# First layer's attention: normalisation and scaling moved to GpSimd, the roots gathered in two slots

## What is computed

```python
xn = layernorm(x) * gamma
q, k, v = split(xn @ w_q, xn @ w_kv)          # 16 heads of 64
k, v = concat(null_k, k), concat(null_v, v)   # two null keys in front
q = q / max(norm(q), 1e-12) * q_scale
k = k / max(norm(k), 1e-12) * k_scale
sim = 8 * q @ k.T + alibi, causal
out = softmax(sim) @ v                        # per head
return concat_heads(out) @ w_out
```

## Time and profile before

| | us |
|---|---|
| median of 3 runs | 2028.43 |
| lowest and highest | 2022.0, 2038.33 |
| the profiled execution | 2043.86 |
| its span from first to last instruction | 2042.1 |

### The profile page before, as it was taken

One profiled execution on the slowest core, in us unless ns is written; L12 is line 12 of the kernel. 1 busy time (PEld: TensorE's weight loads), 2 busy tenths in 40 slices (PEclk: granted clock), 3 DMA queues, 4 the chain that ended last, 5 costly groups with the idle time before them and its releaser, 6 DMA issues. The chain is left out here.

```text
span 2042.1 us, 35995 instructions
## 1 busy us (share of the span) xinstructions
PE 1633.4 (80%) x13931; PEld 819.6 (40%) x13931; DVE 1223.0 (60%) x2150; ACT 886.8 (43%) x1438; POOL 764.7 (37%) x423
## 2 busy tenths in 40 slices
PE   2468459879889898898989998345998889888887
PEld 2246325435354353544535443224654323333232
DVE  5323357686766757576576661481266877777761
ACT  0112215536456463564635455012322655555566
POOL 1500553564656656465564768260000111400000
PEclk9879759989899998999989999567998977888888
DMA  4113210000000000000000000123320000000000
GB/s 156 52 32 107 48 24 12 7 12 22 7 19 11 18 17 7 24 12 12 17 7 20 12 12 12 65 79 94 93 74 27 13 13 28 9 18 2 2 7 17
DMA packets 57109, 62.00 MB, mean 30 GB/s; under 512 B 12890, under 2 KB 42862, under 8 KB 56046
## 3 DMA queue, kind: packets, MB, share of 16 engines
q1 hardware_dynamic: 52846, 51.32, 8.1%
q0 software_dynamic: 4096, 8.40, 1.6%
HBM read 40.34 MB, written 18.48 MB: 29 GB/s over the span
## 5 line engine op out<-in xcount | busy, mean ns | idle before, releaser
L1582 POOL TENSOR_TENSOR a_prob_sum<-a_prob_sum,a_prob 128x1024 f32<-128x1024 f32 (+2 forms) x224 | 499.9, 2232 | 239.1 <-ACT a_prob L1530 218.2
L1530 ACT ACTIVATE a_prob<-a_st,a_table 128x512 f32<-128x512 f32 (+3 forms) x640 | 352.7, 626 | 358.3 <-PE a_st L1408 219.5
L1628 DVE TENSOR_REDUCE a_maxima<-a_ring 128x16 f32<-128x512 f32 (+3 forms) x640 | 352.8, 600 | 127.2 <-PE a_ring L1340 102.5
L1914 DVE TENSOR_REDUCE a_maxima<-a_mx 128x1 f32<-128x512 f32 (+3 forms) x640 | 352.3, 605 | 122.1 <-PE a_mx L1898 59.7
L2158 ACT ACTIVATE a_prob<-a_st 128x1024 f32<-128x1024 f32 (+3 forms) x320 | 269.0, 894 | 183.3 <-PE a_st L2076 102.4
L1435 PE MATMUL a_ot<-a_prob,a_values 128*64 128x512 f32 (+3 forms) x1280 | 289.0, 570 | 0.0
L1340 PE MATMUL a_ring<-a_k_hi,a_q_hi 64*128 64x512 f16 (+3 forms) x640 | 166.1, 373 | 94.2 <-DVE a_maxima L1628 71.6
L1898 PE MATMUL a_mx<-a_ks,a_qs 32*128 32x512 f16 (+3 forms) x640 | 188.3, 393 | 39.9 <-DVE a_maxima L1914 36.7
L2092 PE MATMUL a_ot<-a_prob,values_all 128*32 128x512 f32 (+3 forms) x1280 | 179.8, 638 | 0.2 <-ACT a_sums L2150 0.2
L2041 POOL DMA_INDIRECT a_back<-expert_out,slot_from x32 | 30.3, 948 | 347.7 <-ACT a_prob L2158 347.7
L1898 PEld LDWEIGHTS a_mx<-a_ks,a_qs 32*128 32x128 f16 x640 | 46.4, 93 | 246.8 <-DVE a_maxima L1914 173.8
(11 more groups left out here) (260 smaller groups left out, 2600.2 us busy)
## 6 DMA issues: line engine op xcount, KB each, us to landing
a_rden<-rden_wide SPq DMA_DIRECT2D x64, 128.0 KB, 2.9
f_w<-in_w SPq DMA_DIRECT2D x28, 256.0 KB, 2.8
expert_in<-zeros SPq DMA_DIRECT2D x5, 1024.0 KB, 11.2
f_rows<-expert_in SPq DMA_DIRECT2D x16, 256.0 KB, 3.7
expert_out<-f_result SPq DMA_DIRECT2D x16, 256.0 KB, 2.2
shared_w<-in_w SPq DMA_DIRECT2D x12, 256.0 KB, 3.1
a_table<-in_head_table SPq DMA_DIRECT2D x16, 140.5 KB, 2.2
parts<-part_t SPq DMA_DIRECT2D x4, 512.0 KB
```

Of the source, the lines that this page charges most:

```text
L1530: e = act.activation(prob[:, s % NPROB, a, c0:QW], ps_st[s % 2][:, a, c0:QW], ACT.Exp, bias=table[x][:, a, at:at + 1])
L1582: pool.tensor_tensor(into[:, :, c0:QW], into[:, :, c0:QW], here[:, :, c0:QW], ALU.add).then_inc(added, 2 if r == TPQ - 2 else 1)
L1628: dve.reduce_max(maxima[:, qt // TPQ, a, qt % TPQ, at:at + count], bank[:, 0:hi - lo].rearrange("p (w k) -> p w k", k=WINDOW), AX_X).then_ ...
L1914: dve.reduce_max(own.maxima[:, qt // TPQ, a, qt % TPQ, n:n + 1], bank[:, 0:hi - lo], AX_X).then_inc(done, 1)
```

## The change

Four edits, all in the first layer's attention.

- The normalisation of q and k in the plan `NEXT0` goes from VectorE at slots 25 to 28 to GpSimd: groups 0 and 1 at slot 39 and groups 2 and 3 at slot 3 of the next pair. In the plans of pair 0 it stays on VectorE.
- The roots in `NEXT0` are made in two slots, parts 0 and 1 at slot 23, parts 2 and 3 at slot 24. The first part waits for the normalisations of the pair before.
- `scale_out` goes from VectorE to GpSimd in all pairs, behind the addition of its slot. `invert` waits for the scaling before.
- The q and k units start at slot 9 instead of 11 and the v units at slot 2 instead of 4, with the squares and sums moved along.

```diff
-        self.newton = {qk + 2 * NQB + 2 + k: k for k in range(NEWTON + 1)}
+        self.newton = {qk + 2 * NQB + 2 + k: (k,) for k in range(NEWTON + 1)}
...
-NEXT0 = Ahead0(11)
+NEXT0 = Ahead0(9)
+NEXT0.newton = {ENDS0[2]: (0, 1), ENDS0[2] + 1: (2, 3)}
+POOL_NORM0 = {ENDS0[3]: (0, 1), ENDS0[0]: (2, 3)}
...
-V_AT0 = {4 + u: u for u in range(V_UNITS0)}
+V_AT0 = {2 + u: u for u in range(V_UNITS0)}
...
+            def normalise(pair, g):
+                rows = raw[:, TPQ * g:TPQ * g + TPQ, :].rearrange("p t (g d) -> p t g d", d=DH0)
+                r = rnorm[:, 4 * TPQ * g:4 * TPQ * (g + 1)].rearrange("p (t g) -> p t g", g=4)
+                pool.wait_ge(newton_step, pair * NEWTON_STEPS + NEWTON_STEPS)
+                pool.tensor_tensor(rows, rows, r.unsqueeze(3).to_broadcast([P, TPQ, 4, DH0]), ALU.mult).then_inc(qn_done, 1)
+
+            def scale_out(qb, count):
+
+                pool.wait_ge(rden_loaded, 32 * count + 32)
+                pool.wait_ge(ot_read, count + 1)
+                pool.tensor_tensor(out_t[:, :], out_raw[qb % 2][:, :], rden[:, :], ALU.mult).then_inc(scaled, 1)
+
             def step(i, first=False, last=False):
-                for n in range(2 * NS0):
-                    add(i, n, n // NS0, n % NS0, first, last)
+                for n in range(2 * NS0 + (TAIL0 if last else 0)):
+                    x, s = divmod(n, NS0)
+                    if x < 2:
+                        add(i, n, x, s, first, last)
+                    if s in SCALE_AT0 and is_born(x, SCALE_AT0[s], first):
+                        scale_out(SCALE_AT0[s], i * (2 * NQB) + outs_before(x, SCALE_AT0[s]))
+                    ahead = 2 if s == ENDS0[3] else 1
+                    if x < 2 and x + ahead < (2 if last else 4) and not (first and x + ahead < 3):
+                        for g in POOL_NORM0.get(s, ()):
+                            normalise(2 * i + x + ahead, g)
...
                 if part == 0:
                     dve.wait_ge(ss_done, pair * NQB + NQB)
+                    if not (isinstance(pair, int) and pair == 0):
+                        dve.wait_ge(qn_done, pair * NQB)
...
             def invert(count):
+                if is_past(count):
+                    dve.wait_ge(scaled, count)
                 dve.wait_ge(den_turned, 32 * count + 32)
                 dve.reciprocal(rden_rows[:, :], den_rows[:, :]).then_inc(inverted, 1)
-
-            def scale_out(qb, count):
-
-                dve.wait_ge(rden_loaded, 32 * count + 32)
-                dve.wait_ge(ot_read, count + 1)
-                dve.tensor_tensor(out_t[:, :], out_raw[qb % 2][:, :], rden[:, :], ALU.mult).then_inc(scaled, 1)
...
-                        if s in at.newton:
-                            inverse_roots(2 * i + pair, at.newton[s])
-                        if s in at.norm:
+                        for part in at.newton.get(s, ()):
+                            inverse_roots(2 * i + pair, part)
+                        if at is not NEXT0 and s in at.norm:
                             normalise(2 * i + pair, at.norm[s])
```

More of the change, by code:

```diff
@@ L1708, in step @@
                         invert(i * (2 * NQB) + outs_before(x, INVERT_AT0[s]))
-                    if s in SCALE_AT0 and is_born(x, SCALE_AT0[s], first):
-                        scale_out(SCALE_AT0[s], i * (2 * NQB) + outs_before(x, SCALE_AT0[s]))
                     for unit in one:
```

## The result

The change made the kernel faster by 1.0%: a median of 2019.26 us (2004.37 to 2032.08) against 2039.35 us (2022.0 to 2052.17) for the kernel before in the same sittings, 20 runs each; the ratio is 0.9901 with an interval of 0.9879 to 0.9922. That is 20 us, where 36 were forecast. The forecast's 1992 us stood on the median of the first three runs of before, 2028.43; the twenty put before 11 us higher, so 11 of the 27 us between 1992 and 2019 are its starting point and 16 the change. The profiled execution took 2019.5 us, its span 2017.7; that of before took 2043.86 and 2042.1.

A forecast was written before the change was run, and what follows sets the result against it. TensorE was taken as the bound. A pair gains 3.3 + 4.4 + 0.4 - 1.5 = 6.6 us, 33 in pairs 1 to 5, plus 3 elsewhere: 2028.4 - 36 gives 1992 us, own range 1980 to 2006, with rivals 1968 to 2020.

The forecast's parts named there:

- The bound and the two places: First layer's attention: TensorE is the bound; two places in each of pairs 1 to 5 hold most of its longest wait.
- places A and B: A: slots 21 to 25, roots blocked by GpSimd's add; B: slots 27 to 30, normalisations and scaling blocked among adds.
- Place B, 3.3 + 4.4 us a pair: Slots 27 to 30: the 3.31 us TensorE wait goes, and 4.4 us of slow clock behind it (bounds 0 and 4.4).
- The first rival: The slow clock stays, because new shorter waits in place A and before projections also bring 1.2 GHz; 12 us gained, 2016; chance 0.17.
- Normalisation on GpSimd for nothing: Slots 39 and 3: four normalisations of 1.81 to 2.36 us each fit on GpSimd at no cost, 2.5 us to spare.
- the third rival: GpSimd becomes the bound: projections wait for scaling behind two adds, 1.9 us at each border; 44 us slower, 2072; chance 0.12.
- New waits before the projection, 1.5 us a pair: TensorE waits for GpSimd's scaling: 0.7 us at slot 17, 0.6 at slot 29, none at 5 and 9; 1.5 a pair.
- The moved units and the two waits of VectorE at nothing: Earlier v units, and new waits of the reciprocal for scaling and first root for normalisation, cost nothing.
- Place A, 0.4 us gained: Roots in slots 23 and 24: one wait becomes two shorter ones, 0.4 us gained a pair; bounds 0 and 2.7.
- their 3 us: Pairs 0, 6 and 7 together gain 3 us, from scalings no longer blocked on VectorE, less new waits for GpSimd.
- its best case of 2.7 us: Place A's upper bound, 2.24 + 0.42 us a pair, if the lift of the maxima slips in before the add.
- the second rival: The blocking only moves: roots and lift meet a lagging GpSimd, place A worse by some 3 us a pair; 2007 to 2012; chance 0.08.

The follow-up runs named there:

- kernel with GpSimd's wait: Changed kernel plus one wait: GpSimd's addition of slot 25 waits until the pair's roots are complete; 2003.61 us, ratio 0.9838 to the kernel before.
- kernel with the roots at slot 25: Changed kernel with all four root parts behind slot 25's maxima, and GpSimd's addition of slot 25 waiting for them; 1974.61 us, ratio 0.9688 to the kernel before.

## Why the prediction was right or wrong

**The bound and the two places: right.** The time came and went in places A and B. By the end of the attention the changed kernel is 23.0 us ahead (1253.1 against 1276.1), of which 1.6 stood there already at its beginning; the part behind the attention, with the same code, gives 1.4.

**Place B, 3.3 + 4.4 us a pair: right.** Slots 26 to 31 gave 8.3 us. The wait of 3.31 us is gone, and the clock over the stretch rose from 0.73 to 1.00 in pair 3. In the mean TensorE's idle time there fell from 4.8 to 1.0 us and its busy time from 19.4 to 14.9. The first rival came about in its premise and not in its sum: new waits in place A are followed by slow stretches (below), but place B's own slow clock went.

**Normalisation on GpSimd for nothing: right.** It takes 1.90 us, inside the bounds of 1.81 and 2.36 and nearer to the lower, the product with a broadcast. Two end at 692.21 + 4.09 = 696.3, ahead of TensorE's turning at 697.26; the first of them ends at 694.4. GpSimd ended up with 404 us of work in 603, so the third rival's bound isn't near; its other half, waits before the projection in all four borders, isn't there either.

The rows of this chip say 1.90 us on GpSimd against 1.20 on VectorE for the same normalisation, and that moving both operations took 8.3 us off each pair's slots 26 to 31. The Trainium skill (GPSIMD Engine Reference, section 4.1, Engine selection), which the prediction weighed, keeps such work on VectorE. The measurement decides against it here, since VectorE was the engine for which TensorE waited.

**New waits before the projection, 1.5 us a pair: too large.** They are 0.44 us at slot 17, and none shows at slot 29 of pairs 1 to 5. Slots 0 to 19 grew by 0.9 us in all. In pair 6 the wait is 1.90 us, as computed; pair 7 has 1.90 at slot 17 and 2.45 at slot 29, which the sum hadn't.

**The moved units and the two waits of VectorE at nothing: right**, 0.2 us a pair by the kernel that moves the units back.

**Place A, 0.4 us gained: wrong, and this is the step that failed.** It lost 3.4 us a pair, 3.8 x 5 = 19 us against the forecast; place B and the projections gave back some 1.1 us a pair of that, and pairs 0, 6 and 7 gave 2.0 of their 3 us. So 36 forecast became 21 us over the attention's pairs. Of the 3.4 us, 2.3 are idle time of TensorE (5.4 against 3.1 a pair in slots 22 to 25) and the rest is busy time (10.7 against 9.6 for the same work), at a clock of 0.78 to 0.80 in all five pairs against 0.87 and 1.00 before. Three things in the step didn't hold:

- It computed the chain from the additions before the border only. "Then: lift and maximum 0.6, the two first parts of the roots 1.6 [...] the maxima of slot 24 1.29, the other parts 1.5" runs 5.2 us long beside slots 23 and 24, and the addition of slot 25, which starts as soon as its exponentials are there, isn't in it. It began at 768.80, 0.05 us before the other parts, and their first step took 2.37 us. The kernel with GpSimd's wait shows what the step described ("the wait is turned into two shorter ones behind it"): 1.34 and 1.62 us. So the arithmetic of the chain was sound, and its neighbour was missing. Without the collision TensorE reaches the denominators 4.7 us after the last addition before the border has ended, where the step had 5.5 and before had 5.9.
- The first step, said to take 0.2 us, took 0.98: it met the short addition before the border. The lift, which the step had behind that addition, began in front of it, at 764.63. That is the condition that the step gave for its best case of 2.7 us, and it earned nothing.
- It reckoned no slow clock behind two short waits. Even in the kernel with GpSimd's wait slots 22 to 25 take 13.76 us, and slots 24 and 25 there 10.15 against 4.76 in the kernel with the roots at slot 25. In pair 3 it is 9.52 against 4.76: of these 4.8 us 3.0 are the waits, and the clock of 0.87 stands for 2 x 0.13 x 13.1 = 3.4 us at the lower level, of which half, 1.7, is lost. Pairs 1 and 4, with a clock of 0.76, have twice as much of it and make the mean 5.4. The step had only waits in its sum, and so its lower bound of 0 was wrong as well: with the collision away, place A is still 1.1 us slower than before, and by the means above nearly all of that is busy time at the slower clock.

What happened is the second rival, which had 0.08: the blocking moved, place A became worse by about 3 us a pair, and its 2007 to 2012 us stand for the median of before at 2028.4; less the 20 us measured that would be 2008. Its words had the cause as well (roots that meet a GpSimd that doesn't stand still), except that GpSimd didn't lag: it was early. The chance was too low because the argument asked whether GpSimd would be late and not when its next addition would begin. A step of 0.23 us took 2.25 to 2.38 wherever an addition of some 2.35 began just before it. The Trainium skill (SBUF — State Buffer, section SBUF: two separate sides) has the one that starts second stand for the whole of the other's instruction, and the traces agree. I had used the rule for the additions before the chain and not for the one behind.

**Still open.** The first slots of pair 0 differ by up to 2.5 us between kernels that have the same code there, and pair 0 became 1.8 us longer instead of 2.2 shorter, all of it there by its slot 2, ahead of any moved work; no run explains it. Why the part behind the attention takes 757 to 777 us was not tried. Whether a scaling on VectorE at slot 17 shortens the whole kernel isn't settled. Why TensorE's clock falls isn't settled either: 1.34 and 1.62 us of waiting were followed by clocks of 0.76 and 0.87, the single waits of up to 0.9 us weren't; but with the scaling back on VectorE three pairs fell to 0.90 with no wait over 0.8 us in the stretch, and two stayed at 1.00 with one of 2.39. No kernel varied the waits to find out. Why a normalisation a slot later makes place B 2.4 us longer is open too.

## What to carry to other kernels

Before a chain of short operations goes into a gap of another engine, look up when that engine's next operation becomes ready, not only when its last one ends; if the chain is longer than the gap, let that engine wait for the chain's end, provided that it has time to spare. An engine that is off the critical path and has slack is the one on which to put the wait. Costs of blocking don't add up: either of two blocked operations alone cost some 2 us a pair here, both together 8.3. So the first of them to be moved, whichever it is, looks worth 6 to 7 us and the second 2; judge them by all four combinations and not by one at a time.

## What the runs showed of the hardware

- An added semaphore wait made the kernel faster twice: by 2.7 us a pair with the roots in slots 23 and 24, and by 6.8 with the roots at slot 25.
- A chain of dependent VectorE steps of 0.2 us doesn't hold off GpSimd: an addition gets in between two of them. The kernel without the wait lost 2.26 and 2.38 us to two additions that began in its chain.
- Five pairs in a row, 561.7 us, ran at a granted clock of 1.00 once the last long waits were gone; in the kernel before the same pairs showed 0.96 over 622.6 us. By those rows 2 x 0.04 x 622.6 = 50 us were at the lower level; half of them, 25 us, is the most that the clock can have cost of the 60.9 us between the two.
- The granted clock didn't follow the longest wait alone: with the scaling back on VectorE, slots 26 to 31 had a wait of 2.39 us and a clock of 1.00 in pairs 2 and 4, and no wait over 0.8 us and a clock of 0.90 in pairs 1, 3 and 5.
- GpSimd's product with a broadcast operand takes 1.90 us for 1024 columns (1896 ns at the lowest, 2235 at the highest of 20), its addition of the same size 2.35.
